# Attention exponentials turned by DMA instead of by TensorE in a pipelined attention and feed-forward block

## The chip, the cores and the metric

The kernel runs on one core of a Trainium2 chip. The metric is the device time of one execution in microseconds; lower is better. Before the change three runs gave 545.62, 542.62 and 543.9 us, median 543.9 us.

## The reference

There are 16 batches of 512 rows with 128 features. Per batch:

```python
x = x + _layernorm(attn(_layernorm(x)))      # attn: scores = (x*w_lhs) @ (x*w_rhs).T, softmax over rows, @ x
x = x + _layernorm(ffn(_layernorm(x)))
# ffn: h = silu(x@w1*s1) * (x@w2*s2)         128 -> 512
#      h = gelu(h@h1*sh1); h = gelu(h@h2*sh2)  512 -> 512 -> 512
#      y = h@w3*s3                            512 -> 128
```

The weights w1, w2, h1, h2 and w3 are ternary, all tensors are float32.

## The kernel before, in words

**Numbers in two halves.** A float32 value is kept as a high half and a low half, low = value - high. The feed-forward matmuls take fp32r halves, the product of attention weights and x takes fp16 halves. Each pair costs one rounding (the high half) and one subtraction on VectorE (the low half).

**Software pipeline.** Batches overlap. In step i five batches are at work (class `Stages`): `prep` = i+1 gets its first layer norm and is turned to features-first, `att` = i runs attention, `mid` = i-1 gets its second layer norm and is turned, `ffn` = i-2 runs the hidden layers, `tail` = i-3 runs the last layer and is stored. Attention of batches 0 and 1 is in `start()`, the last two batches' hidden layers in `finish()`. Steps 2 and 3 are written out, steps 4 to 14 are a loop, step 15 is written out. In the rest of the text a is the batch in attention, b the one in `mid`, f in `ffn`, g in `tail`.

**Order.** Nothing schedules the work but the text of the kernel: every engine has its own `step()` that lists its operations by hand, engines meet by semaphores, and an engine that waits holds all that is behind it. What the steps below need:

- TensorE (`pe`): `scores(a, j)` makes 128 query rows by 512 keys into one of two PSUM banks, `score_bank[j % 2]`, j = 0 to 3; it waits until `exp_done` says that the bank's earlier rows were read. `turn_e(a, j)` turns the 128 x 512 exponentials with four fp32 transposes into `eT_bank`. `attend(a, j)` multiplies them with x. `turn_x`, `turn_x2` and `turn_y` turn other tensors. `gated`, `layer1`, `layer2` and `layer3` are the feed-forward layers. Near the end of a step stand `attend(a, 0)`, `turn_e(a, 3)`, `turn_x2(b)`, `attend(a, 1)`, the last two `layer2` matmuls, `attend(a, 2)` and `attend(a, 3)`.
- ScalarE (`act`): `softmax(a, j)` is one Exp from the score bank to `exps` in float32, with the row sum. `high_e(a, j)` copies `eT_bank` to `eT_hi` (fp16). `silu`, `gelu1`, `gelu2`: the gelus are evaluated twice from PSUM, once for the value and once for the high half.
- VectorE (`dve`): `row_max(a, j)` on the scores, `low_e(a, j)` = `eT_bank` - `eT_hi`, one operand in PSUM, one in SBUF. `high_A` and `low_A` round and split the gated product, `low_B` and `low_C` split the gelus; these take both operands from SBUF. `aggregate(ln_x, prep)` finishes the statistics that GpSimd waits for.
- GpSimd (`pool`): in each step and in this order, `high_xn`, `rstd(ln_x)` and `normalize_x(prep)`, `rstd(ln_y)` and `shift_x1(g)`, `rstd(ln_x1)` and `normalize_x1(b)` which writes `x2n` for `turn_x2`, and the attention norm's constants. An `rstd` is four small operations that wait for each other: `var_eps`, `rstd` (a power of -0.5), `scaled_mean`, `shift`. In the profile ln_x1's tensors are shown as ln_x_..., x1 as x.
- SyncE (`sp`): loads of x, the store, and x1 saved and loaded again, one queue.

## Time and profile before

| | |
|---|---|
| median of three runs | 543.9 us (542.62 to 545.62) |
| span of the profiled execution | 548.2 us |
| that execution's time outside the profile | the records hold none; the three times above are the runs' |
| TensorE busy | 485.0 us (88%) |
| VectorE busy | 430.9 us (79%) |
| ScalarE busy | 393.2 us (72%) |
| GpSimd busy | 283.5 us (52%) |
| DMA, share of 16 engines | 12.6% |

Busy shares are means over stages, and TensorE's matmuls overlap each other in the records, so their starts tell more than their lengths. L12 is line 12 of the kernel. An operation is written "out<-in". "ISA" and "REGISTER_ALU" rows in listings of the program's order are waits and their register sums.

### The profile page before, as it was taken

Reading aid. Unit: us, or ns where it says so; the run is one execution under the profiler, and the core shown is the slowest. Engines: PE = TensorE matmul, PEld = TensorE weight load, DVE = VectorE, ACT = ScalarE, POOL = GpSimd, SP = SyncE. Lnnn points to the kernel's source line nnn. Section 1 sums busy time; section 2 is a strip of 40 time slices with the busy share of each in tenths; the row PEclk is TensorE's granted clock in tenths of the full one; section 3 lists DMA queues with packets and bytes.
Section 4 is the critical chain, followed back from the end, with each engine's and each line's share of the span. In section 5 each row is a group of like instructions: output and inputs, shape, how many; then the busy total and the mean of one; then the engine's idle time right before and its main releaser. Section 6 shows DMA issues by size and latency. Waiting matters only on the chain.

```text
span 548.2 us, 10143 instructions
## 1 busy us (share of the span) xinstructions
PE 485.0 (88%) x2818; PEld 386.8 (71%) x2818; DVE 430.9 (79%) x1160; ACT 393.2 (72%) x657; POOL 283.5 (52%) x568
## 2 busy tenths in 40 slices
PE   0765999999899989989898998989899998999992
PEld 0544777777777768777786877777777776877781
DVE  2873969889797978879697987969698797878762
ACT  3673777878697777868686786878678686875861
POOL 5364143837555472755547384655638365255332
PEclk9977999999999999999999999999999999999997
DMA  7010010100302020020202011020201102020111
GB/s 269 19 50 13 20 59 1 62 37 0 97 0 96 0 96 0 18 77 0 96 0 96 0 40 56 0 96 0 96 0 57 38 0 77 1 77 2 38 39 38
DMA packets 12549, 24.13 MB, mean 44 GB/s; under 512 B 1520, under 2 KB 1520, under 8 KB 12528
## 3 DMA queue, kind: packets, MB, share of 16 engines
q1 hardware_dynamic: 12528, 23.87, 12.6%
q8 instruction: 11, 0.18, 0.1%
q14 instruction: 10, 0.08, 0.0%
HBM read 11.28 MB, written 4.19 MB: 28 GB/s over the span
## 4 chain that ended last, share of the span: by engine, by line
PE 42%; POOL 30%; issue 14%; DVE 9%; ACT 2%; POOLq 2%; DMA 0%; DVEq 0%; SPq 0%
PE hid_bank L353 13%; PE hid_bank L277 10%; POOL x2n L1100 6%; PE score_bank L277 5%; POOL ln_x_rstd L1083 5%; PE mix_bank L277 5%; PE eT_bank L375 5%; POOL xn L1100 4%; POOL w_raw L1095 3%; POOL ln_y_rstd L1083 3%; POOL ln_x_shift L1088 2%; PE score_bank L282 2%; DVE hA_lo L777 2%; POOL ln_y_var_eps L1079 2%; POOL ln_x_scaled_mean L1085 2%
## 5 line engine op out<-in xcount | busy, mean ns | idle before, releaser
L628 ACT ACTIVATE w_raw<-hid_bank,columns 128x512 f32<-128x512 f32 x128 | 88.7, 693 | 25.6 <-PE hid_bank L353 21.0
L353 PE MATMUL hid_bank<-hA_hi,w_hi 128*128 128x512 f32 x256 | 104.6, 409 | 0.4 <-DVE w_raw L805 0.4
L353 PE MATMUL hid_bank<-hB_hi,w_hi 128*128 128x512 f32 x256 | 104.7, 409 | 0.0
L353 PE MATMUL hid_bank<-hA_lo,w_hi 128*128 128x512 f32 x256 | 101.0, 395 | 0.0
L353 PE MATMUL hid_bank<-hB_lo,w_hi 128*128 128x512 f32 x256 | 100.9, 394 | 0.0
L618 ACT ACTIVATE w_raw<-hid_bank,columns 128x512 f32<-128x512 f32 x64 | 43.6, 684 | 40.2 <-PE hid_bank L277 40.2
L777 DVE TENSOR_TENSOR hC_lo<-w_raw,hC_hi 128x512 fp32r<-128x512 f32 x64 | 45.7, 716 | 22.7 <-ACT hC_hi L629 22.6
L610 ACT CAST eT_hi<-eT_bank 128x512 f16<-128x512 f32 x64 | 37.9, 593 | 33.1 <-PE eT_bank L282 32.6
L1079 POOL TENSOR_SCALAR ln_x_var_eps<-ln_x_mean_var 128x4 f32<-128x4 f32 x32 | 9.5, 297 | 99.3 <-DVE ln_x_mean_var L790 98.0
L277 PE MATMUL hid_bank<-x2T_hi,w_hi 128*128 128x512 f32 x128 | 54.5, 426 | 3.7 <-issue 3.2
L805 DVE SCALAR_TENSOR_TENSOR w_raw<-hid_bank,columns,w_raw 128x512 f32<-128x512 f32 x64 | 47.7, 745 | 11.8 <-ACT w_raw L618 11.8
L353 PEld LDWEIGHTS hid_bank<-hA_hi,w_hi 128*128 128x128 f32 x256 | 48.2, 188 | 12.0 <-DVE w_raw L805 1.2
L353 PEld LDWEIGHTS hid_bank<-hB_hi,w_hi 128*128 128x128 f32 x256 | 48.2, 188 | 9.6
L353 PEld LDWEIGHTS hid_bank<-hB_lo,w_hi 128*128 128x128 f32 x256 | 48.3, 189 | 9.3
L777 DVE TENSOR_TENSOR hB_lo<-w_raw,hB_hi 128x512 fp32r<-128x512 f32 x64 | 45.7, 713 | 11.5 <-ACT hB_hi L629 11.5
L353 PEld LDWEIGHTS hid_bank<-hA_lo,w_hi 128*128 128x128 f32 x256 | 48.3, 189 | 8.8
L604 ACT ACTIVATE exps<-score_bank,neg_max 128x512 f32<-128x512 f32 x64 | 43.9, 687 | 13.7 <-DVE neg_max L795 10.9
L277 PE MATMUL hid_bank<-x2T_lo,w_hi 128*128 128x512 f32 x128 | 51.2, 400 | 2.5 <-issue 2.5
L777 DVE TENSOR_TENSOR eT_lo<-eT_bank,eT_hi 128x512 f16<-128x512 f32 x64 | 43.6, 681 | 4.4 <-ACT eT_hi L610 4.3
L282 PE MATMUL eT_bank<-ident,exps 128*128 128x128 f32 x256 | 40.1, 280 | 7.3 <-ACT exps L604 3.9
L277 PE MATMUL mix_bank<-xn_hi,eT_hi 128*128 128x128 f16 x256 | 46.3, 222 | 0.2 <-DVE eT_lo L777 0.2
L277 PE MATMUL mix_bank<-xn_hi,eT_lo 128*128 128x128 f16 x256 | 45.9, 220 | 0.0
(85 smaller groups left out, 1229.3 us busy)
## 6 DMA issues: line engine op xcount, KB each, us to landing
x_in<-x_dram SPq DMA_DIRECT2D x16, 256.0 KB, 2.8
x_res<-x_dram SPq DMA_DIRECT2D x16, 256.0 KB, 2.7
x_all<-x SPq DMA_DIRECT2D x16, 256.0 KB, 2.3
x_tail<-x_all SPq DMA_DIRECT2D x16, 256.0 KB, 2.8
out_dram<-w_raw SPq DMA_DIRECT2D x16, 256.0 KB, 2.0
w_raw<-weights_dram SPq DMA_DIRECT2D x5, 512.0 KB, 5.9
w_raw<-weights_dram SPq DMA_DIRECT2D x1, 256.0 KB, 7.3
columns<-columns_dram SPq DMA_DIRECT2D x1, 9.5 KB, 2.4
```

What stands on the lines that cost most here:

```text
L277: mm = nc.tensor.matmul(out, lhs, rhs, start=(n == 0), stop=(n == len(pairs) - 1))
L282: mm = nc.tensor.transpose(bank[:, t * P:(t + 1) * P], src[:, t * P:(t + 1) * P], ident[:, :])
L353: mm = nc.tensor.matmul(hid_bank[m][:, :], lhs, rhs, start=(k == 0 and n == 0), stop=(k == K - 1 and n == len(pairs) - 1))
L375: mm = nc.tensor.matmul(w3_bank[:, :], lhs, rhs, start=(k == 0 and n == 0), stop=(k == K - 1 and n == len(pairs) - 1))
L604: nc.scalar.activation(exps[:, j, :], score_bank[j % 2][:, :], ACT.Exp, bias=neg_max[:, j:j + 1], scale=-1.0, accum_out=row_sum[:, j:j + 1 ...
L610: nc.scalar.copy(eT_hi[:, j, :, :].rearrange("p t s -> p (t s)"), eT_bank[:, :]).then_inc(eT_hi_ready, 1)
L618: nc.scalar.activation(gate[:, m % 2, :], hid_bank[2 * (m % 2)][:, :], ACT.Silu, scale=columns[:, S1 + m:S1 + m + 1]).then_inc(gate_ready, 1)
L628: nc.scalar.activation(h_full[:, m, :], hid_bank[m][:, :], ACT.Gelu, scale=scale)
L777: return nc.vector.tensor_tensor(out, a, b, ALU.subtract)
L805: nc.vector.scalar_tensor_tensor(h_full[:, m, :], hid_bank[2 * (m % 2) + 1][:, :], columns[:, S2 + m:S2 + m + 1], gate[:, m % 2, :], ALU.m ...
L1083: nc.gpsimd.tensor_tensor(norm.rstd[:, :], norm.var_eps[:, :], minus_half[:, :], ALU.pow).then_inc(norm.chain, 1)
L1100: op = nc.gpsimd.tensor_scalar(out[:, t, :], src[:, t, :], norm.rstd[:, t:t + 1], norm.shift[:, t:t + 1], ALU.mult, ALU.add)
```

## The change

The exponentials are no longer turned by TensorE. ScalarE evaluates Exp twice from the score bank: once to fp16 (the high half, half 0 of `e_split`), once to float32 (`exps`, with the row sum). VectorE subtracts them, both from SBUF, to half 1 of `e_split`. Then SyncE's queue turns both halves of 128 x 512 at once with a DMA transpose of 128 x 1024 fp16 (256 KB) into `eT`, and `attend` waits for its landing. `eT_bank` and `high_e` are gone, and the bank is layer 3's alone. The order of SyncE and VectorE is written anew. The gated product is rounded and split by VectorE as before.

```diff
-        eT_hi = sb("eT_hi", [P, T, T, P], f16)
-        eT_lo = sb("eT_lo", [P, T, T, P], f16)
+        e_split = sb("e_split", [P, T, 2, S], f16)
+        eT = sb("eT", [P, T, 2, T, P], f16)
...
+            def turn_e(a, j):
+                sp.wait_ge(e_lo_ready, a * T + j + 1)
+                apart(sp)
+                wait_free(sp, pv_done, T, a, j + 1 - T)
+                apart(sp)
+                sp.dma_start_transpose(eT[:, j, :, :, :].rearrange("p h t s -> p (h t) s"),
+                                       e_split[:, j, :, :].rearrange("p h s -> p (h s)")).then_inc(eT_landed[j], 16)
...
-            def turn_e(b, j):
-                pe.wait_ge(exp_done, b * T + j + 1)
-                if j == 0:
-                    wait_free(pe, yT_ready, 1, b, -2)
-                wait_free(pe, eT_lo_ready, T, b, j)
-                turn(eT_bank, exps[:, j, :], eT_turned)
...
-                pe.wait_ge(eT_lo_ready, b * T + j + 1)
+                pe.wait_ge(eT_landed[j], b * 16 + 16)
...
-                wait_free(act, eT_turned, T, b, j + 1 - T)
+                wait_free(act, e_lo_ready, T, b, j + 1 - T)
                 if j == 0:
                     wait_free(act, rs_chain, 2, b, -1)
+                wait_free(act, eT_landed[j], 16, b, 0)
+                nc.scalar.activation(e_split[:, j, 0, :], score_bank[j % 2][:, :], ACT.Exp, bias=neg_max[:, j:j + 1],
+                                     scale=-1.0)
                 nc.scalar.activation(exps[:, j, :], score_bank[j % 2][:, :], ACT.Exp, bias=neg_max[:, j:j + 1],
                                      scale=-1.0, accum_out=row_sum[:, j:j + 1]).then_inc(exp_done, 1)
-
-            def high_e(b, j):
-                act.wait_ge(eT_turned, b * T + j + 1)
-                wait_free(act, pv_done, T, b, j + 1 - T)
-                nc.scalar.copy(eT_hi[:, j, :, :].rearrange("p t s -> p (t s)"), eT_bank[:, :]).then_inc(eT_hi_ready, 1)
...
             def low_e(b, j):
-                dve.wait_ge(eT_hi_ready, b * T + j + 1)
-                minus(eT_lo[:, j, :, :].rearrange("p t s -> p (t s)"), eT_bank[:, :],
-                      eT_hi[:, j, :, :].rearrange("p t s -> p (t s)")).then_inc(eT_lo_ready, 1)
+                dve.wait_ge(exp_done, b * T + j + 1)
+                minus(e_split[:, j, 1, :], exps[:, j, :], e_split[:, j, 0, :]).then_inc(e_lo_ready, 1)
```

**VectorE in a full step**, from the row maximum of j = 2 to the first `low_B`. Before (low_e is `eT_lo`, x1's statistics are ln_x_stats<-x):

```order
L795 TENSOR_REDUCE neg_max<-score_bank 128x1
L777 TENSOR_TENSOR hA_lo<-w_raw,hA_hi 128x512
L813 CAST hA_hi<-w_raw 128x512
L795 TENSOR_REDUCE neg_max<-score_bank 128x1
L790 BN_AGGR ln_x_mean_var<-ln_x_stats 128x2 x4
L777 TENSOR_TENSOR hA_lo<-w_raw,hA_hi 128x512
L849 SCALAR_TENSOR_TENSOR x<-mix_bank,ln_att_rstd,att_base 128x128 x4
L777 TENSOR_TENSOR xn_lo<-xn,xn_hi 128x512
L777 TENSOR_TENSOR eT_lo<-eT_bank,eT_hi 128x512
L782 BN_STATS ln_y_stats<-mix_bank 128x6 x4
L777 TENSOR_TENSOR hB_lo<-w_raw,hB_hi 128x512
```

Now, the same stretch (low_e is `e_split`):

```order
L777 TENSOR_REDUCE neg_max<-score_bank 128x1
L794 CAST hA_hi<-w_raw 128x512
L777 TENSOR_REDUCE neg_max<-score_bank 128x1
L759 TENSOR_TENSOR hA_lo<-w_raw,hA_hi 128x512
L772 BN_AGGR ln_x_mean_var<-ln_x_stats 128x2 x4
L759 TENSOR_TENSOR e_split<-exps,e_split 128x512
L830 SCALAR_TENSOR_TENSOR x<-mix_bank,ln_att_rstd,att_base 128x128 x4
L759 TENSOR_TENSOR e_split<-exps,e_split 128x512
L759 TENSOR_TENSOR xn_lo<-xn,xn_hi 128x512
L759 TENSOR_TENSOR e_split<-exps,e_split 128x512
L764 BN_STATS ln_y_stats<-mix_bank 128x6 x4
L759 TENSOR_TENSOR hB_lo<-w_raw,hB_hi 128x512
```

`aggregate(ln_x)` moved behind the last `low_A`, and three of the four `low_e` now stand between it and the first `low_B` (the fourth stands behind the second `low_B`); before, one did.

**ScalarE in a full step**, from Exp's table to the first gelu. Before:

```order
L604 ACT_TABLE_LOAD
L604 ACTIVATE exps,row_sum<-score_bank,neg_max 128x512 x2
L642 ACTIVATE w_raw<-eT_bank,columns 128x512
L604 ACTIVATE exps,row_sum<-score_bank,neg_max 128x512
L610 CAST eT_hi<-eT_bank 128x512
L604 ACTIVATE exps,row_sum<-score_bank,neg_max 128x512
L628 ACT_TABLE_LOAD
```

Now:

```order
L605 ACT_TABLE_LOAD
L605 ACTIVATE e_split<-score_bank,neg_max 128x512
L607 ACTIVATE exps,row_sum<-score_bank,neg_max 128x512
L605 ACTIVATE e_split<-score_bank,neg_max 128x512
L607 ACTIVATE exps,row_sum<-score_bank,neg_max 128x512
L640 ACTIVATE w_raw<-w_bank,columns 128x512
L605 ACTIVATE e_split<-score_bank,neg_max 128x512
L607 ACTIVATE exps,row_sum<-score_bank,neg_max 128x512
L605 ACTIVATE e_split<-score_bank,neg_max 128x512
L607 ACTIVATE exps,row_sum<-score_bank,neg_max 128x512
L626 ACT_TABLE_LOAD
```

All eight evaluations stand ahead of the gelu table; the copies that stood among the gelus are gone.

**SyncE in the loop's body.** Before:

```order
L226 DMA x_tail<-x_all 128x512
L229 REGISTER_ALU
L230 DMA out_dram<-w_raw 128x512
L221 ISA
L221 DMA x_all<-x 128x512
L217 ISA
L217 DMA x_res<-x_dram 128x512
```

Now:

```order
L217 DMA x_res<-x_dram 128x512
L233 ISA
L185 REGISTER_ALU
L237 DMA_TRANSPOSE eT<-e_split 128x8x128
L221 ISA
L221 DMA x_all<-x 128x512
L233 REGISTER_ALU
L185 REGISTER_ALU
L237 DMA_TRANSPOSE eT<-e_split 128x8x128
```

Two more transposes and the store follow. The store, which waits for the tail's result, is now last, and x1's save stands behind the first transpose.

## Rows read from the trace of the kernel before

**Rows 1.** The page: busy time of the engines, and the chain that ended last, by engine

```profile
PE 485.0 (88%) x2818; PEld 386.8 (71%) x2818; DVE 430.9 (79%) x1160; ACT 393.2 (72%) x657; POOL 283.5 (52%) x568
...
PE 42%; POOL 30%; issue 14%; DVE 9%; ACT 2%; POOLq 2%; DMA 0%; DVEq 0%; SPq 0%
```

**Rows 2.** ScalarE's timeline, silu table loads of steps 3 and 15: start, length (us)

```profile
82.42 1.28 ACT L615 ACT_TABLE_LOAD   x1
...
460.62 1.28 ACT L615 ACT_TABLE_LOAD   x1
```

**Rows 3.** Busy time of each engine in one full step

```profile
238.80:270.46 31.66, 29.59 (x180) 23.79 (x178) 26.46 (x72) 23.95 (x41) 17.89 (x35) 1.00 0.12 41
```

**Rows 4.** TensorE's timeline in that step: start, length; in brackets idle time and releaser

```profile
249.40 0.40 PE L277 MATMUL score_bank<-xT_hi,aT_lo 128*128 128x512 f32 x1
...
260.68 0.60 PE L282 MATMUL eT_bank<-ident,exps 128*128 128x128 f32 x4
...
261.04 0.47 PE L353 MATMUL hid_bank<-hB_hi,w_hi 128*128 128x512 f32 x1
...
265.07 0.61 PE L282 MATMUL eT_bank<-ident,exps 128*128 128x128 f32 x4
...
267.48 0.63 PE L282 MATMUL score_bank<-ident,x2n 128*128 128x128 f32 x4 [1.80 <-POOL x2n L1100]
```

**Rows 5.** Waits: engine, tile and line, releaser: total us, times, longest

```profile
PE score_bank L282 <- POOL x2n L1100: 20.5, 13, 1.8
```

**Rows 6.** VectorE's timeline in that step

```profile
250.21 0.68 DVE L795 TENSOR_REDUCE neg_max<-score_bank 128x1 f32<-128x512 f32 x1
...
250.81 0.37 DVE L790 BATCH_NORM_AGGREGATE ln_x_mean_var<-ln_x_stats 128x2 f32<-128x6 f32 x4
...
251.10 0.66 DVE L777 TENSOR_TENSOR hA_lo<-w_raw,hA_hi 128x512 fp32r<-128x512 f32 x1
...
252.71 0.68 DVE L777 TENSOR_TENSOR xn_lo<-xn,xn_hi 128x512 f16<-128x512 f32 x1
...
253.31 0.68 DVE L777 TENSOR_TENSOR eT_lo<-eT_bank,eT_hi 128x512 f16<-128x512 f32 x1
...
254.77 0.84 DVE L777 TENSOR_TENSOR hB_lo<-w_raw,hB_hi 128x512 fp32r<-128x512 f32 x1
...
256.88 0.69 DVE L777 TENSOR_TENSOR hB_lo<-w_raw,hB_hi 128x512 fp32r<-128x512 f32 x1 [0.40 <-ACT hB_hi L629]
...
258.27 0.68 DVE L777 TENSOR_TENSOR eT_lo<-eT_bank,eT_hi 128x512 f16<-128x512 f32 x1
```

**Rows 7.** GpSimd's timeline in that step

```profile
251.38 0.43 POOL L1079 TENSOR_SCALAR ln_x_var_eps<-ln_x_mean_var 128x4 f32<-128x4 f32 x1 [5.66 <-DVE ln_x_mean_var L790]
...
252.99 0.46 POOL L1085 TENSOR_TENSOR ln_x_scaled_mean<-ln_x_mean_var,ln_x_rstd 128x4 f32<-128x4 f32 x1
...
254.18 2.62 POOL L1100 TENSOR_SCALAR xn<-x_in,ln_x_rstd,ln_x_shift 128x128 f32<-128x128 f32 x4 [0.34 <-POOL ln_x_shift L1088]
...
256.88 0.74 POOL L1079 TENSOR_SCALAR ln_y_var_eps<-ln_y_mean_var 128x4 f32<-128x4 f32 x1
...
258.81 0.20 POOL L1085 TENSOR_TENSOR ln_y_scaled_mean<-ln_y_mean_var,ln_y_rstd 128x4 f32<-128x4 f32 x1
...
264.60 2.63 POOL L1100 TENSOR_SCALAR x2n<-x,ln_x_rstd,ln_x_shift 128x128 f32<-128x128 f32 x4 [0.31 <-POOL ln_x_shift L1088]
```

**Rows 8.** GpSimd's timeline in the start: the same four operations of xn

```profile
37.64 1.74 POOL L1100 TENSOR_SCALAR xn<-x_in,ln_x_rstd,ln_x_shift 128x128 f32<-128x128 f32 x4 [0.34 <-POOL ln_x_shift L1088]
```

**Rows 9.** ScalarE's timeline in that step, then its group of copies (busy, mean ns | idle)

```profile
246.67 0.69 ACT L604 ACTIVATE exps<-score_bank,neg_max 128x512 f32<-128x512 f32 x1
...
247.25 0.19 ACT L604 ACTIVATION_READ_ACCUMULATOR exps<-score_bank,neg_max 128x1 f32 x1
...
L610 ACT CAST eT_hi<-eT_bank 128x512 f16<-128x512 f32 x64 | 37.9, 593 | 33.1 <-PE eT_bank L282 32.6
```

**Rows 10.** DMA issues: KB each, median us from issue to landing

```profile
x_in<-x_dram SPq DMA_DIRECT2D x16, 256.0 KB, 2.8
...
w_raw<-weights_dram SPq DMA_DIRECT2D x1, 256.0 KB, 7.3
```

**Rows 11.** VectorE's timeline in the start: attention statistics of batch 0

```profile
28.82 0.89 DVE L782 BATCH_NORM_STATS2 ln_att_stats<-mix_bank 128x6 f32<-128x128 f32 x4
```

134 lines of the change are left out of this document (59 added, 75 removed).

## The prediction

> **What bounds the kernel now.** I read the page first. TensorE is busy 88% of the span, VectorE 79%, ScalarE 72%, GpSimd 52% [rows 1]. That suggests TensorE, and taking transposes from it would then pay at once. The chain that ended last says otherwise in the same rows: TensorE has 42% of it and GpSimd, the idlest, 30%. So I looked at one step. The silu table loads of steps 3 to 15 begin 378.2 us apart over 12 steps [rows 2], 31.5 us a step, and steps 5 to 14 look alike; the one from 238.80 to 270.46 took 31.66 us, with TensorE's records covering 29.59 [rows 3]. These 12 steps are two thirds of the time.
>
> In that step TensorE stands still at one place worth the name. It finishes `turn_e(a, 3)`, issued at 265.07, and then waits 1.80 us for `x2n` before `turn_x2` at 267.48 [rows 4]; over the kernel that wait counts 20.5 us in 13 times [rows 5]. Follow `x2n` back. GpSimd starts at 251.38, after 5.66 us of idleness that `aggregate(ln_x)` ends, and then runs ln_x, xn, ln_y, the tail's base, ln_x1 and `x2n` with no gap until 264.60 + 2.63 = 267.23 [rows 7]: 15.85 us in a row. `aggregate(ln_x)` begins at 250.81, right behind the last row maximum at 250.21 [rows 6], which needs the scores whose last matmul TensorE issued at 249.40 [rows 4]. So the loop is: TensorE from the step's start to the last scores (238.80 to 249.63, 10.8 us), VectorE (to 251.38, 1.75 us), GpSimd (15.85 us), TensorE's `turn_x2`, three `attend` and two matmuls (267.48 to 270.46, 3.0 us), and 0.25 us of hand-over. That is the step's 31.66. **None of the four `turn_e` lies in this loop**: the first follows the last scores, the last stands before the wait.
>
> **What is taken away.** One `turn_e` costs TensorE 0.36 us, from its start to the next instruction's (260.68 to 261.04) [rows 4]. Four are 1.44 us a step. They come off a stretch that ends in the 1.80 us of waiting, so the wait grows to about 3.2 us and the gain is 0. The cover is GpSimd's chain; if it went, 1.44 us a step would be paid out. `high_e`, four copies a step of 593 ns [rows 9], leaves ScalarE; in the steady step ScalarE waits there for TensorE, so nothing is gained.
>
> **What ScalarE gets.** One Exp holds ScalarE for 0.58 us (246.67 to the accumulator's read at 247.25 [rows 9]), and each `exp_done` now comes after two. The first comes 0.6 us later, so `scores(a, 2)` waits some 0.3 us, and `scores(a, 3)`, which needs the second, ends 0.4 us later in all. VectorE came late to that maximum anyway: the scores' last matmul was issued at 249.40 and takes 0.40 [rows 4], the maximum began at 250.21 [rows 6], 0.4 us after it. So only about 0.05 us reach the maximum.
>
> **What VectorE's new order costs.** `low_A(f, 3)` now stands ahead of `aggregate(ln_x)`. Such a subtraction holds VectorE for 0.60 us (252.71 to 253.31) [rows 6]. That delay goes into GpSimd's chain whole: **+0.6 us** a step, +0.65 with the 0.05.
>
> **What the new operands cost GpSimd.** This the diff hides. `low_e` took one operand from PSUM; now it takes both from SBUF. Compare the small operations of GpSimd, 0.20 us when undisturbed (258.81, while VectorE runs an `eT_lo` from PSUM since 258.27) [rows 6, 7]. `ln_x_scaled_mean` took 0.46 us while `xn_lo` ran from SBUF, and ended with it; `ln_y_var_eps` took 0.74 us beside an `hB_lo` that began in the same instant, 256.88 [rows 6, 7]. The four operations of `xn` took 2.62 us with two `hB_lo` beside them [rows 7], and 1.74 us undisturbed [rows 8]: 0.44 us lost per subtraction. The Trainium skill has this as a rule (SBUF — State Buffer, "Who interferes with whom"): a VectorE instruction with two SBUF inputs and a GpSimd instruction that reads SBUF exclude each other for the whole instruction, and one with at most one SBUF input does not. By that rule, the trace agrees, all four `low_e` change sides. They will stand at about 251.9, 253.5, 254.7 and 257.7 of that step's clock, all inside GpSimd's 15.85 us.
>
> The price of the four lies between two ends. The upper is 4 x 0.44 = 1.8 us a step. The lower is a small gain, -0.35 us: a `low_e` that falls on the 1.02 us power operations costs nothing, and they push the `hB_lo` to other places than the `var_eps` at 256.88 and the `shift` behind it, where two of these now cost 0.5 us each. Laid against the chain by hand: the first takes the place that `hA_lo` had, behind `aggregate`, where it costs the same 0.23 us; the second meets `scaled_mean` as `xn_lo` did; `xn_lo` then meets `shift`, +0.2; the third and the `hB_lo` cost `xn` up to 0.5 more; `ln_y` gets back up to 0.6; `x2n` meets the same two `hC_lo`, with one `shift` about 0.2 worse. I take **+0.25 us**, near the lower end, since the hand-laid order is the nearest thing to evidence. Sum per full step: 0.65 + 0.25 = **+0.9 us**, ends +0.3 and +2.4. Twelve steps: **+10.8 us** (+4 to +29).
>
> **What the transposes cost.** No row shows a DMA transpose. A plain load of the same 256 KB lands 2.8 us after issue; the slowest of that size 7.3 us, queued behind five others [rows 10]. I take about 3 us, nearest to the lone transfers. In the step there is room: the last `low_e` ends near 258.4, the last `attend` comes after 269. Moving x1's save behind the first transpose, and the store to the end of SyncE's queue, hides too: the save's data is needed two steps later, and the next load of x stood behind the store before, too.
>
> **Start and ends.** In the start there is no cover. All of batch 0's exponentials must be subtracted and landed before `attend(0, 3)`; before, that batch's statistics began at 28.82 [rows 11]. VectorE will be done with the subtractions near 25, plus 3 us, plus two `scores` of batch 1 that now stand ahead of the attends, 0.7 to 1.5 us each at that point: about 31. I put down **+2.5 us**, ends 0 and +6 (the latter if four transposes in a row need 2 us each on the queue). Step 2 waits at its first `layer2` for ScalarE, which reaches the gelus 1.1 us later (four Exps of 0.58, less one copy, and less waits), and gets two or three `turn_e` back: +0.5. Step 15 has no `prep`, and its chain runs over `turn_y`, whose statistics now stand behind three `low_e`: +0.7. `finish()` is unchanged.
>
> **Sum.** 10.8 + 2.5 + 0.5 + 0.7 = 14.5 us, on the profiled execution's span of 548.2 us: 562.7. The median of the runs is 543.9, so I forecast **558 us** in their terms; the 4.3 us between them stay.
>
> **Rivals.**
>
> *TensorE pays out.* If GpSimd's chain isn't the bound after all, or shrinks under the new order, the 1.44 us count: up to 14 x 1.44 = 20 us, **524 us**. For it: TensorE is busy 29.59 of 31.66 us [rows 3]. Against it: the wait of 1.80 us in 13 of the steps [rows 5], and nothing in the diff shortens GpSimd's 15.85. It decides as soon as `aggregate(ln_x)` to `x2n` gets shorter than 15.2 us, 0.65 less than now. 0.13.
>
> *The ports cost the upper end.* Each of the four `low_e` stops GpSimd for 0.44 us: +2.4 us a step, 29 us and 3.7 for the rest, **577 us**. For it: the rows of `xn` with and without company [rows 7, 8]. Against: the power operations are untouched. 0.12.
>
> *The transposes are slow.* Four must run between the end of the first `low_e`, near 252.6, and the last `attend`, near 269.9: from 4.3 us each, one after another, they become the bound. At the 7.3 us of [rows 10] they'd end at 281.8, 11.9 us late, 12 times 11.9 on 543.9: **687 us**. Against: that row is a transfer behind others. 0.07. The Trainium skill speaks against the change here (VectorE: DVE Perf Modes, "The three transpose paths"): 1309 ns by DMA against 390 ns on TensorE for 128 x 128 of two bytes; if eight such blocks added up, one transpose would take 10.5 us and the time would be some 700 us, an estimate from that page. No row here shows it.
>
> *Nothing to measure.* The hand-laid gains in ln_y cancel the 0.65: **544 us**. 0.10.
>
> The forecast itself has 0.58, with its own range of 547 to 570.
>
> **How the numbers follow.** A measurement here tells about 0.5% (2.7 us) from no change. Slower: 0.58 + 0.12 + 0.07 = 0.77, less 0.01 for the forecast's lower edge = 0.76. Same: 0.10, and that 0.01, 0.11. Faster: 0.13. The range of 541 to 577 leaves out the payout of TensorE and the slow transposes, 0.20.
>
> **What would show it.** Right: full steps of 32.3 to 33 us; the wait of TensorE on `x2n` up from 1.8 to about 3; GpSimd's chain from `ln_x_var_eps` to the end of `x2n` over 15.85 us, with small operations of 0.4 to 0.75 us beside `e_split`; `aggregate(ln_x)` 0.6 us later in the step. Wrong: steps under 31.5 us, a wait of TensorE on a DMA ahead of `attend`, `scores(a, 3)` late by over 1 us, or a GpSimd chain no longer than before.

## The result, and the profile after

The changed kernel takes 592.05 us, median of four runs (591.05 to 594.01), beside 544.66 us for the kernel before on the same chip (542.62 to 545.62): ratio 1.0865, 95% interval 1.0805 to 1.0925. The forecast was 558 us, with a range that ended at 577. The sign was right, and the loss is three times what was forecast: 47 us instead of 14.

The page of the changed kernel: busy time, the clock granted to TensorE in 40 slices, and the chain that ended last.

```profile
PE 487.1 (82%) x2562; PEld 374.1 (63%) x2562; DVE 427.9 (72%) x1160; ACT 392.9 (66%) x657; POOL 298.5 (50%) x568
...
PEclk9876879999797999989799998999798999999997
...
PE 37%; POOL 22%; issue 18%; DVE 12%; ACT 9%; POOLq 1%; ACTq 1%; DVEq 0%; DMA 0%; SPq 0%
```

Set against [rows 1] two things stand out. TensorE issues 256 matmuls fewer and is yet busy 2 us longer, and GpSimd, to which the change gave nothing to do, is busy 15 us longer. DMA has no share of the chain.

ScalarE's timeline gives the steps, as in [rows 2]: the silu table loads of steps 3 and 15.

```profile
94.38 1.28 ACT L613 ACT_TABLE_LOAD   x1
...
503.22 1.28 ACT L613 ACT_TABLE_LOAD   x1
```

The twelve full steps take 34.07 us each ((503.22 - 94.38) / 12), 2.55 more than in the profile of before; the forecast was 0.9 more. Together they are 30.6 of the 44.0 us between the two profiled executions. The start takes 7.8 us more (first silu table load at 52.78 instead of 44.97), step 2 takes 4.15 more and step 15 takes 1.4 more.

The view by windows: three full steps and a part of a fourth. Columns as in [rows 3]: busy time of PE, PEld, DVE, ACT and POOL, granted clock, DMA share, GB/s.

```profile
94.38:127.58 33.20, 28.85 (x162) 21.98 (x162) 26.37 (x72) 24.03 (x41) 19.47 (x35) 1.00 0.30 72
127.58:162.21 34.63, 31.21 (x162) 24.08 (x162) 26.22 (x72) 23.84 (x41) 18.17 (x35) 0.90 0.29 69
...
299.05:332.55 33.50, 28.66 (x162) 21.99 (x162) 26.38 (x72) 23.96 (x41) 19.33 (x35) 1.00 0.29 70
...
286.00:290.00 4.00, 4.00 (x12) 3.32 (x12) 1.85 (x4) 1.18 (x2) 3.23 (x8) 0.50 0.19 34
```

So there are two kinds of step. In the shorter one TensorE runs at its full clock throughout, the 2.4 GHz level, and the step is still 1.8 us longer than the one of [rows 3], with GpSimd busy 19.33 us instead of 17.89. In the longer one the granted clock falls to 0.50, the 1.2 GHz level, for some microseconds.

**The shorter kind.** VectorE's timeline of the step 299.05 to 332.55, from the last row maximum on:

```profile
310.53 0.69 DVE L777 TENSOR_REDUCE neg_max<-score_bank 128x1 f32<-128x512 f32 x1 [0.26 <-PE score_bank L299]
...
311.74 0.37 DVE L772 BATCH_NORM_AGGREGATE ln_x_mean_var<-ln_x_stats 128x2 f32<-128x6 f32 x4
...
313.64 0.68 DVE L759 TENSOR_TENSOR e_split<-exps,e_split 128x512 f16<-128x512 f32 x1
314.24 0.68 DVE L759 TENSOR_TENSOR xn_lo<-xn,xn_hi 128x512 f16<-128x512 f32 x1
314.85 0.68 DVE L759 TENSOR_TENSOR e_split<-exps,e_split 128x512 f16<-128x512 f32 x1
...
317.13 0.65 DVE L759 TENSOR_TENSOR hB_lo<-w_raw,hB_hi 128x512 fp32r<-128x512 f32 x1
317.71 0.68 DVE L759 TENSOR_TENSOR e_split<-exps,e_split 128x512 f16<-128x512 f32 x1
318.31 0.68 DVE L759 TENSOR_TENSOR hB_lo<-w_raw,hB_hi 128x512 fp32r<-128x512 f32 x1
```

GpSimd's timeline beside it:

```profile
312.31 0.43 POOL L1060 TENSOR_SCALAR ln_x_var_eps<-ln_x_mean_var 128x4 f32<-128x4 f32 x1 [6.50 <-DVE ln_x_mean_var L772]
...
313.93 1.66 POOL L1066 TENSOR_TENSOR ln_x_scaled_mean<-ln_x_mean_var,ln_x_rstd 128x4 f32<-128x4 f32 x1
...
316.32 3.68 POOL L1081 TENSOR_SCALAR xn<-x_in,ln_x_rstd,ln_x_shift 128x128 f32<-128x128 f32 x4 [0.34 <-POOL ln_x_shift L1069]
...
326.63 2.54 POOL L1081 TENSOR_SCALAR x2n<-x,ln_x_rstd,ln_x_shift 128x128 f32<-128x128 f32 x4 [0.31 <-POOL ln_x_shift L1069]
```

`ln_x_scaled_mean`, an operation of 0.20 us when undisturbed, took 0.46 in [rows 7] and takes 1.66 here. It was ready at 313.93 and ends at 315.59, just after the last of three subtractions that stand back to back from 313.64 to about 315.45. Three more such subtractions, 317.13 to 319.0, stand inside `xn`, which takes 3.68 us instead of 2.62 [rows 7] or 1.74 undisturbed [rows 8]. The whole chain, from `ln_x_var_eps` to the end of `x2n`, takes 16.86 us (312.31 to 329.17), 1.01 us more than before.

What TensorE waits for, in all of the kernel:

```profile
PE score_bank L304 <- POOL xn L1081: 58.1, 16, 11.5
...
PE score_bank L304 <- POOL x2n L1081: 12.5, 7, 3.0
PE hid_bank L368 <- DVE hB_lo L759: 10.3, 14, 0.7
```

The wait for `x2n` of [rows 5] has shrunk. In its place TensorE now waits at `turn_x` for `xn`, a place where it lost almost nothing before.

**The longer kind.** TensorE's timeline around `turn_x`, of the step 264.67 to 299.05 (mean clock 0.90) and, in the last line, of the step at 299.05; start and length, idle time in brackets:

```profile
285.77 1.11 PE L304 MATMUL score_bank<-ident,xn 128*128 128x128 f32 x4 [2.39 <-POOL xn L1081]
286.53 0.78 PE L368 MATMUL hid_bank<-hB_hi,w_hi 128*128 128x512 f32 x1
287.10 0.63 PE L368 MATMUL hid_bank<-hB_lo,w_hi 128*128 128x512 f32 x1
287.53 0.63 PE L368 MATMUL hid_bank<-hB_hi,w_hi 128*128 128x512 f32 x1
...
320.15 0.65 PE L304 MATMUL score_bank<-ident,xn 128*128 128x128 f32 x4 [2.38 <-POOL xn L1081]
```

In the step at 299.05 the same wait is 2.38 us, and behind it these matmuls start 0.23 us apart; here they start 0.43 us apart. Around `turn_x` the two steps differ in what the clock did after equal waits. The Trainium skill says that TensorE's clock falls to half when the engine is idle (TensorE: Matmul & The Clock Gate, "What's actually happening"). The trace agrees that the fall follows idle time, and it adds that equal waits of 2.4 us here bring the fall in some steps and not in others.

The DMA rows, issue to landing and then SyncE's own timeline:

```profile
eT<-e_split SPq DMA_TRANSPOSE x64, 3.1
```

```profile
312.95 1.27 SPq L237 DMA_TRANSPOSE eT<-e_split  x1
```

A transpose lands 3.1 us after its issue (forecast: about 3) and holds the queue for about 1.25 us. No wait of TensorE on a DMA stands among those of the page.

One remark on the profile of before. Its full steps come in two lengths too: two of the twelve take 30.7 us and the rest 31.7, all at full clock. Its span of 548.2 us is an execution on the long side, so differences of steps to it come out somewhat small. I judge versions by the ratio of their times, and use the lengths of steps to find the place.

### The profile page after: what moved, and what is told of

The parts are those of the page before. It is cut to its first block, busy times and chain, and to the rows that moved or that the text cites. A ratio compares the mean times of both kernels' runs of the same rounds, so it can differ in the third digit from the quotient of the medians.

```text
span 592.2 us, 9780 instructions
## 1 busy us (share of the span) xinstructions
PE 487.1 (82%) x2562; PEld 374.1 (63%) x2562; DVE 427.9 (72%) x1160; ACT 392.9 (66%) x657; POOL 298.5 (50%) x568
## 4 chain that ended last, share of the span: by engine, by line
PE 37%; POOL 22%; issue 18%; DVE 12%; ACT 9%; POOLq 1%; ACTq 1%; DVEq 0%; DMA 0%; SPq 0%
PE hid_bank L368 20%; PE score_bank L299 6%; DVE w_raw L786 4%; POOL xn L1081 4%; POOL ln_x_scaled_mean L1066 4%; POOL ln_x_rstd L1064 4%; PE mix_bank L299 4%; PE score_bank L304 3%; PE hid_bank L299 3%; POOL x2n L1081 2%; ACT L613 2%; DVE hA_lo L759 2%; ACT hC_hi L627 2%; POOL ln_y_rstd L1064 2%; ACT e_split L605 1%
## 5 line engine op out<-in xcount | busy, mean ns | idle before, releaser
L368 PE MATMUL hid_bank<-hB_hi,w_hi 128*128 128x512 f32 x256 | 115.7, 452 | 10.3 <-DVE hB_lo L759 10.3
L368 PE MATMUL hid_bank<-hB_lo,w_hi 128*128 128x512 f32 x256 | 110.8, 433 | 0.0
L368 PEld LDWEIGHTS hid_bank<-hB_hi,w_hi 128*128 128x128 f32 x256 | 55.5, 217 | 27.9 <-ACT hB_hi L627 14.9
L304 PE MATMUL score_bank<-ident,xn 128*128 128x128 f32 x64 | 15.4, 386 | 58.1 <-POOL xn L1081 58.1
L368 PEld LDWEIGHTS hid_bank<-hB_lo,w_hi 128*128 128x128 f32 x256 | 54.9, 215 | 11.5
L1081 POOL TENSOR_SCALAR xn<-x_in,ln_x_rstd,ln_x_shift 128x128 f32<-128x128 f32 x64 | 57.5, 907 | 5.4 <-POOL ln_x_shift L1069 5.4
L299 PE MATMUL mix_bank<-xn_hi,eT 128*128 128x128 f16 x512 | 52.2, 224 | 0.0
L304 PEld LDWEIGHTS score_bank<-ident,xn 128*128 128x128 f32 x64 | 9.9, 191 | 64.6 <-issue 42.4
L605 ACT ACTIVATE e_split<-score_bank,neg_max 128x512 f16<-128x512 f32 x64 | 44.0, 687 | 8.8 <-DVE neg_max L777 8.0
L777 DVE TENSOR_REDUCE neg_max<-score_bank 128x1 f32<-128x512 f32 x64 | 43.6, 683 | 6.6 <-PE score_bank L299 6.3
```

The costliest lines, as they stand in the source:

```text
L299: mm = nc.tensor.matmul(out, lhs, rhs, start=(n == 0), stop=(n == len(pairs) - 1))
L304: mm = nc.tensor.transpose(bank[:, t * P:(t + 1) * P], src[:, t * P:(t + 1) * P], ident[:, :])
L368: mm = nc.tensor.matmul(hid_bank[m][:, :], lhs, rhs, start=(k == 0 and n == 0), stop=(k == K - 1 and n == len(pairs) - 1))
L605: nc.scalar.activation(e_split[:, j, 0, :], score_bank[j % 2][:, :], ACT.Exp, bias=neg_max[:, j:j + 1], scale=-1.0)
L777: nc.vector.tensor_reduce(neg_max[:, j:j + 1], score_bank[j % 2][:, :], AX.X, ALU.min).then_inc(max_ready, 1)
L1081: op = nc.gpsimd.tensor_scalar(out[:, t, :], src[:, t, :], norm.rstd[:, t:t + 1], norm.shift[:, t:t + 1], ALU.mult, ALU.add)
```

## The experiments

A step's length below is the distance between silu table loads of a steady stretch. "Ratio" is to the kernel before on the same chip, with its 95% interval.

**1. One operand instead of two** (`e1_low_e_one_operand`)

```diff
-                minus(e_split[:, j, 1, :], exps[:, j, :], e_split[:, j, 0, :]).then_inc(e_lo_ready, 1)
+                nc.vector.tensor_reduce(e_junk[:, j:j + 1], exps[:, j, :], AX.X, ALU.min).then_inc(e_lo_ready, 1)
```

> The changed kernel, with each low_e replaced by a row minimum of exps: one operand from SBUF, about the same 0.68 us on VectorE, in the same place; the low half of the exponentials is left out (zeros). Theory A (VectorE instructions with two SBUF operands, back to back, shut GpSimd out: ln_x_scaled_mean 1.66 us and xn 3.68 us for four): scaled_mean falls to about 0.5, xn to about 2.7, xn is ready 2 us sooner, TensorE's wait before turn_x shrinks below 1 us, its granted clock stays at 1.00 in all full steps, and a full step takes 31.9 to 32.6 us instead of 34.1: some 565 us in all. Theory B (the moved aggregate and ScalarE's eight evaluations in a row make the loss): nothing changes by over 0.3 us a step, 590 us. Theory C (the DMA transposes make it): 590 us too.

Measured: 552.54 us, ratio 1.0105 (1.0056 to 1.0153). The same order, the same transposes, the same ScalarE, VectorE as busy as ever, and the loss shrinks from 8.65% to 1.05%. Full steps take 31.0 us at clock 1.00. Of the 7.6 points some 1.5 are the start and step 2, which get 7.9 us shorter in the profile. GpSimd's timeline in this run:

```profile
316.56 0.19 POOL L1061 TENSOR_SCALAR ln_x_var_eps<-ln_x_mean_var 128x4 f32<-128x4 f32 x1 [6.49 <-DVE ln_x_mean_var L773]
...
317.93 0.20 POOL L1067 TENSOR_TENSOR ln_x_scaled_mean<-ln_x_mean_var,ln_x_rstd 128x4 f32<-128x4 f32 x1
...
319.36 2.17 POOL L1082 TENSOR_SCALAR xn<-x_in,ln_x_rstd,ln_x_shift 128x128 f32<-128x128 f32 x4 [0.83 <-DVE xn_lo L760]
...
328.53 2.38 POOL L1082 TENSOR_SCALAR x2n<-x,ln_x_rstd,ln_x_shift 128x128 f32<-128x128 f32 x4 [0.31 <-POOL ln_x_shift L1070]
```

The chain takes 14.35 us (316.56 to 330.91). So four VectorE subtractions with two SBUF operands are what the loss hangs on; the transposes and the second Exp, which this run keeps, leave it at 1.05%. The row minimum differs from the subtraction in one more thing: it writes 128 numbers and not 128 x 512. Experiment 10 excludes that as the reason: there `low_e` writes as much as ever and has one operand in PSUM, and `xn` is undisturbed.

**2. The operand alone, in the kernel before** (`e3_before_two_sbuf`)

```diff
-                minus(eT_lo[:, j, :, :].rearrange("p t s -> p (t s)"), eT_bank[:, :],
+                minus(eT_lo[:, j, :, :].rearrange("p t s -> p (t s)"), exps[:, j, :],
```

> The kernel before, with low_e reading exps from SBUF instead of the transposed exponentials from PSUM, nothing else; the low halves are of the wrong values. The four low_e stand apart there. Theory A: each that meets GpSimd's chain at anything but a power operation costs it up to 0.6 us; the first (behind xn_lo, before a shift) and the second (before ln_y's scaled_mean) and the third (before ln_x1's scaled_mean) do: +0.5 to +1.5 us a step, 551 to 563 us. Theory B and C: 544 us.

Measured: 559.93 us, ratio 1.0222 (1.0175 to 1.0268), full steps of 32.06 us, GpSimd busy 18.94 us of one against 17.89 in [rows 3]. The same four operands from SBUF, spread as the kernel before spreads `low_e`, cost a quarter of what the change costs. GpSimd's chain in such a step takes 16.27 us. `ln_x_scaled_mean` takes 1.06 us there, beside `xn_lo` and a `low_e` in a row. This kernel subtracts the wrong values; its operations are of the same kind and size.

**3. The order alone, in the kernel before** (`e2_before_aggregate_later`)

```diff
-                if st.prep is not None:
-                    aggregate(ln_x, st.prep)
                 if f is not None:
                     low_A(f, 3)
+                if st.prep is not None:
+                    aggregate(ln_x, st.prep)
```

> The kernel before with one move of the change alone: aggregate(ln_x) behind the last low_A. The prediction priced this move at 0.6 us a full step, since it goes into GpSimd's chain whole: 7 us in all, ratio 1.010 to 1.015. Rival (the chain is no bound, or the moved operations rearrange GpSimd's collisions to its good): ratio 0.998 to 1.004.

Measured: 545.17 us, ratio 1.0001 (0.9976 to 1.0025). The forecast's largest term, 0.6 us a step, is nothing. GpSimd's timeline in this run, first and last operation of its chain:

```profile
312.95 0.20 POOL L1079 TENSOR_SCALAR ln_x_var_eps<-ln_x_mean_var 128x4 f32<-128x4 f32 x1 [6.25 <-DVE ln_x_mean_var L790]
...
325.06 2.56 POOL L1100 TENSOR_SCALAR x2n<-x,ln_x_rstd,ln_x_shift 128x128 f32<-128x128 f32 x4 [0.31 <-POOL ln_x_shift L1088]
```

The chain begins 0.6 us later in the step and takes 14.67 us (312.95 to 327.62) instead of 15.85: `hA_lo` is over before `ln_x_var_eps` begins (0.20 us, 0.43 in [rows 7]), and other collisions move as well.

**4. The place of `turn_x`** (`e4_turn_x_later`). 

```diff
                         layer2(general, f, (0,), (0,))
-                    if st.prep is not None:
-                        turn_x(st.prep)
...
                         layer2(general, f, (3,), (0,))
+                    if st.prep is not None:
+                        turn_x(st.prep)
```

> The changed kernel, with TensorE's turn_x of the next batch moved behind the 14 layer-2 matmuls that follow it in the order (3.3 us of work that does not need it). If TensorE's idle time there halves its clock in two steps of three and the slow stretch costs about 1 us a step (34.5 against 33.5 us), all full steps come to 33.5 us or a little less and the granted clock to 1.00: 7 to 9 us less, 583 us. If the clock falls for another reason, or x2n is all that counts, the time stays at 592 us.

Measured: 600.23 us, ratio 1.0969 (1.092 to 1.1019), slower than the changed kernel. The wait at `turn_x` is gone, and in the step looked at the one at `turn_x2` is 2.60 us, with the clock at 0.50 soon behind it.

**5. VectorE's order of before** (`e5_order_of_before`). The changed kernel with VectorE's `step()` in the order of the kernel before, which stands in the rows of order ahead of the prediction.

> The changed kernel with VectorE's order in the steps as before the change: aggregate(ln_x) ahead of the last low_A, one low_e behind low_xn, the others spread. The start keeps the new order. Theory A: with no three two-operand subtractions in a row, scaled_mean falls to 0.5 to 0.7 us, xn to 2.6 to 3, and the chain starts 0.7 us sooner; full steps of 31.8 to 32.8 us, 562 to 572 us. Theory B (ScalarE's evaluations): steps stay over 33.5 us. Theory C (the transposes): the last low_e now ends near the end of the step, so attend(a, 3) would wait for a landing 3 us behind it, and steps get longer than 34 us.

Measured: 601.46 us, ratio 1.1000 (1.0947 to 1.1053). The expectations of experiments 4 and 5 both failed, and both runs are slower than the changed kernel. TensorE's idle time had for the most part moved, from `turn_x` to `turn_x2`, and the clock fell there. From the timeline of TensorE in the run with the order of before:

```profile
329.95 1.09 PE L304 MATMUL score_bank<-ident,x2n 128*128 128x128 f32 x4 [2.82 <-POOL x2n L1081]
...
332.08 0.78 PE L368 MATMUL hid_bank<-hB_hi,w_hi 128*128 128x512 f32 x1
```

One `attend` and the two `layer2` matmuls behind it take 1.25 us and 1.00 us here, in the shorter step at 299.05 0.65 and 0.54 us. That made the clock a suspect of its own.

**6. TensorE kept busy ahead of `turn_x`** (`e10_tensore_kept_busy`)

```diff
+                wait_free(pe, exp_done, T, b, -1)
+                for _ in range(fill):
+                    nc.tensor.matmul(xT_bank[:, :], w_hi[:, 0:P], w_hi[:, 0:S], start=True, stop=True)
                 pe.wait_ge(xn_ready, b + 1)
-                wait_free(pe, exp_done, T, b, -1)
```

> The changed kernel with nine more matmuls of constants, 128x512, 0.23 us each, into the bank of turn_x while TensorE would wait for xn. They compute nothing that is used. Theory (in two of three steps the idle time ahead of turn_x lowers the granted clock to 0.50 for about 7 us and costs some 1 us): the granted clock stays 1.00 in the stretch behind turn_x, all full steps take about 33.5 us, 7 to 9 us less than the changed kernel, ratio 1.070 to 1.076. Rival (the clock's fall is covered by the wait for x2n and costs nothing): ratio 1.083 to 1.090, with the wait for x2n longer by what the clock gives back.

Measured: 582.31 us, ratio 1.0723 (1.0677 to 1.0769), as the theory had it. All full steps take 33.42 us, at clock 1.00:

```profile
290.82:324.24 33.42, 30.71 (x171) 23.70 (x171) 26.37 (x72) 23.97 (x41) 19.23 (x35) 1.00 0.29 71
```

1.4 points of the loss are the clock's: 34.07 - 33.42 = 0.65 us a step. GpSimd's chain in this run, first and last operation:

```profile
304.09 0.43 POOL L1062 TENSOR_SCALAR ln_x_var_eps<-ln_x_mean_var 128x4 f32<-128x4 f32 x1 [6.50 <-DVE ln_x_mean_var L774]
...
318.41 2.45 POOL L1083 TENSOR_SCALAR x2n<-x,ln_x_rstd,ln_x_shift 128x128 f32<-128x128 f32 x4 [0.31 <-POOL ln_x_shift L1071]
```

It takes 16.77 us, 2.42 more than in experiment 1, and the step is 2.42 us longer than there, both at clock 1.00. So the four operands' price reaches the step by way of this chain, and whole.

**7. The transposes doubled** (`e7_transposes_doubled`). 

```diff
+                sp.wait_ge(eT_landed[j], a * 32 + 16)
+                apart(sp)
+                sp.dma_start_transpose(eT[:, j, :, :, :].rearrange("p h t s -> p (h t) s"),
+                                       e_split[:, j, :, :].rearrange("p h s -> p (h s)")).then_inc(eT_landed[j], 16)
...
-                pe.wait_ge(eT_landed[j], b * 16 + 16)
+                pe.wait_ge(eT_landed[j], b * 32 + 32)
```

> The changed kernel with every DMA transpose done twice, one after the other, the second waiting for the first. Theory (the transposes are hidden behind other work in a full step): each row block lands 3.2 to 4.5 us later and the last still before its attend, so full steps change by less than 0.3 us; only the start grows, by 4 to 13 us, ratio to before 1.09 to 1.11. Rival (the transposes or SyncE's queue bound the step): steps longer by 3 us or more, ratio above 1.15.

Measured: 658.49 us, ratio 1.2124 (1.2071 to 1.2176), steps of 37.3 us. The expectation was wrong by its own arithmetic. Two in series hold the queue for about 4.7 us, so four pairs need some 19 us, and no more than that lies between the first transpose (312.95) and the last `attend` (331.7) of the changed kernel, with x1's save in the same queue. The wait is there to see:

```profile
PEld mix_bank L303 <- DMA eT<-e_split: 55.3, 22, 3.7
```

So this run tells how much room there is, not that the transposes bind: single ones are issued in 6.8 us (312.95 to 319.79), and the last lands near 321.7, ten microseconds ahead of its `attend`.

**8. An earlier aggregate, in the changed kernel and in the one before** (`e8_aggregate_early`, `e9_before_aggregate_early`). Both orders have `aggregate(ln_x)` right behind `x_statistics` and `low_xn` ahead of the last row maximum; the first also spreads `low_e` among operations on PSUM. Common to both, in VectorE's `step()`:

```diff
                     x_statistics(st.prep)
+                    aggregate(ln_x, st.prep)
                 if a is not None:
                     row_max(a, 2)
+                    low_xn(a)
```

> The changed kernel with VectorE's step in another order: aggregate(ln_x) right behind x_statistics and low_xn ahead of the third row maximum, so that GpSimd starts some 2.4 us earlier in the step, and the subtractions with two SBUF operands alternate with operations on PSUM. Theory (GpSimd's chain, lengthened by VectorE's subtractions from SBUF, sets the step): the chain ends about 2.4 us or more earlier, the waits of TensorE for xn and x2n nearly go, and the step falls from 34.07 us to what TensorE needs, 29.8 to 30.8 us; the whole kernel 540 to 556 us beside 548 before on one chip, ratio 0.985 to 1.015. Rival (the transposes by DMA or their issue on SyncE's queue set the step): the steps stay above 33 us, ratio 1.07 or more.

> The kernel before with the same two moves (aggregate(ln_x) behind x_statistics, low_xn ahead of the third row maximum; low_e stays from PSUM). If GpSimd's chain bounds the kernel before, as the prediction said, the wait of 1.8 us for x2n nearly goes: steps of 29.9 to 30.6 us, 12 to 22 us less in all, ratio 0.96 to 0.98. The rival that TensorE's own work is the bound: ratio 0.995 to 1.005. It also tells what freeing TensorE of four turn_e is worth where GpSimd's chain is no bound: then the other kernel of this call should have steps shorter than this one's by up to 1.44 us.

Measured: 577.17 us, ratio 1.0625 (1.0582 to 1.0669), steps of 33.25 us; and 540.71 us, ratio 0.9933 (0.9906 to 0.9960), steps of 30.72 us. Neither is in its expected range. The second **is faster than both kernels**, by 0.7% on the one before: its gain is real but a third of the least that was expected. With the chain begun 2 us earlier in the step TensorE still waits at `turn_x2`, since the chain got longer: `ln_x_rstd` and `ln_x_shift` collide now (1.67 and 0.73 us), and GpSimd waits 1.85 us for `ln_y`'s statistics. In the first the wait at `turn_x2` is 2.69 us, and 1.4 us after its end the clock falls to 0.50.

**9. The start alone** (`e13_start_reordered`). VectorE, TensorE and SyncE in another order ahead of step 2: `low_e` interleaved, the load of x behind two transposes, attends ahead of the next batch's scores.

> The changed kernel with another order in the start alone, on VectorE, TensorE and SyncE: the two low_e of batch 0 that can come early do, the next load of x stands behind two of its transposes, its attends ahead of batch 1's scores, its attention statistics ahead of two weight splits, and batch 1's attends ahead of turn_x2. Theory (of the 12 us that start and step 2 lost, 4 to 5 are order, 3 are GpSimd shut out by four subtractions in a row): 5 to 9 us less than the changed kernel, ratio to before 1.069 to 1.078, the first silu table load at 44 to 48 us instead of 52.8. Rival (the start loses by the transposes' own time, issue 1.25 us each and 3.1 us to land): 0 to 2 us less, ratio 1.083 to 1.087.

Measured: 587.25 us, ratio 1.0762 (1.0700 to 1.0824). The first silu table load comes at 49.75 instead of 52.78 and step 2 takes 38.6 instead of 41.6 us. Five to six of the twelve microseconds are the order's, the low end of what was expected; the table load was expected at 44 to 48.

**10. The exponentials kept in PSUM** (`e12_exps_in_psum`, `e11_statistics_first`). Both have experiment 9's start and a VectorE order of their own. The scores wait for `low_e` to free their bank. The edit of the operand:

```diff
-                nc.scalar.activation(exps[:, j, :], score_bank[j % 2][:, :], ACT.Exp, bias=neg_max[:, j:j + 1],
+                nc.scalar.activation(score_bank[j % 2][:, :], score_bank[j % 2][:, :], ACT.Exp, bias=neg_max[:, j:j + 1],
...
-                minus(e_split[:, j, 1, :], exps[:, j, :], e_split[:, j, 0, :]).then_inc(e_lo_ready, 1)
+                minus(e_split[:, j, 1, :], score_bank[j % 2][:, :], e_split[:, j, 0, :]).then_inc(e_lo_ready, 1)
```

> The changed kernel with that start, and with the float32 exponentials written back over the scores in their PSUM bank, so that low_e has one operand in SBUF; the bank comes free only after low_e, so low_e stands early in VectorE's step. x_statistics and aggregate(ln_x) stand ahead of the last row maximum. Theory (the port that VectorE's two-operand subtractions share with GpSimd is the main loss): GpSimd's small operations and xn are as short as in the kernel before, full steps of 30.0 to 31.2 us, 535 to 550 us beside 545 before, ratio 0.985 to 1.01. Rival (the time is lost by the longer way from scores to exponentials or by the transposes): steps above 32.5 us, ratio above 1.03.

> As the run with the exponentials in PSUM, with x_statistics at the very start of VectorE's step and aggregate(ln_x) ahead of the first low_e, so that GpSimd's chain starts 4 us earlier than in the changed kernel. If GpSimd's chain is then no bound, TensorE's work of about 28.9 us and the waits between it and ScalarE set the step: 29.5 to 30.5 us, ratio 0.965 to 0.99. If the 0.8 us ahead of the gated products goes into TensorE's first layer whole, steps of 30.5 to 31.2 us, ratio 0.99 to 1.0.

Measured: 584.94 us, ratio 1.0719 (1.0656 to 1.0783), and 585.08 us, ratio 1.0725 (1.0663 to 1.0787), steps of 34.1 us in both, outside both expected ranges. The theory's first half held: GpSimd is busy 17.06 us a step instead of 19.33, and `xn` takes 1.75 us, as undisturbed. The second half fell: the step is no shorter. In the first run GpSimd's chain begins hardly earlier (13.1 us after TensorE's start of the step instead of 13.4), since `scores(a, 2)` waits 0.94 us for `low_e` now; GpSimd then waits 1.44 us for `ln_y`'s statistics. In the second the chain begins 3 us earlier than in the first, waits 3.73 us for the same statistics, and nothing is gained. So `x2n` comes late enough for this (the first run: windows, then TensorE's timeline):

```profile
286.86:321.00 34.14, 30.19 (x162) 23.04 (x162) 26.43 (x72) 23.96 (x40) 17.06 (x35) 0.95 0.28 69
316.40:318.50 2.10, 2.09 (x16) 2.04 (x17) 0.27 (x1) 0.58 (x1) 0.19 (x1) 0.50 0.00 1
```

```profile
316.41 1.09 PE L303 MATMUL score_bank<-ident,x2n 128*128 128x128 f32 x4 [2.70 <-POOL x2n L1093]
```

**11. The same, with TensorE kept busy ahead of `turn_x2`** (`e17_busy_before_turn_x2`). 

```diff
+                for _ in range(fill):
+                    nc.tensor.matmul(x2T_bank[:, :], w_hi[:, 0:P], w_hi[:, 0:S], start=True, stop=True)
+                pe.wait_ge(x2n_ready, b + 1)
```

> The run with the exponentials in PSUM (ratio 1.072, steps 34.13 us), with nine more matmuls of constants, 128x512, 0.23 us each, where TensorE waits 2.70 us for x2n. They compute nothing that is used. Theory (what the change takes from TensorE lengthens that wait, the granted clock then falls to 0.5 and the attends and the first gated matmuls behind it take twice as long): the clock stays 1.00 and the steps fall by 1.2 to 2.0 us, ratio 1.028 to 1.045. Rival (the fall of the clock is covered by another chain): less than 0.4 us a step, ratio 1.063 to 1.075.

Measured: 569.32 us, ratio 1.0410 (1.0378 to 1.0442), steps of 32.54 us. `x2n` is as late as before, and the step is 1.6 us shorter all the same:

```profile
309.17 2.30 PE L338 MATMUL score_bank<-w_hi 128*128 128x512 f32 x9
311.87 0.66 PE L303 MATMUL score_bank<-ident,x2n 128*128 128x128 f32 x4 [0.41 <-POOL x2n L1095]
```

```profile
282.51:315.05 32.54, 30.88 (x171) 23.40 (x171) 26.43 (x72) 23.99 (x41) 17.09 (x35) 1.00 0.29 73
```

**12. The same fill under the order of before** (`e19_order_of_before_kept_busy`): experiment 5 with that edit.

> The run with VectorE's step order of the kernel before (ratio 1.100, steps 34.5 us), with nine idle matmuls of 0.23 us where TensorE waits 2.82 us for x2n. If that run missed its expectation because of the clock granted after that wait (attends and first gated matmuls at 0.5), as the runs on the changed kernel and with the exponentials in PSUM suggest, the steps fall by 1.2 to 1.8 us to 32.7 to 33.3 us, ratio 1.055 to 1.075. If it missed because the subtractions from SBUF cost GpSimd as much in this order too, and the clock is covered, ratio 1.09 to 1.105.

Measured: 582.73 us, ratio 1.0662 (1.0625 to 1.0699), steps of 33.27 us instead of 34.7. So 1.4 us of experiment 5's miss was the clock. The rest of it stands: 31.8 to 32.8 us had been expected, and with the clock at full in both, the order of before is about as good as the change's own (1.0662 against 1.0723, each with the fill at its place; the intervals overlap). GpSimd's chain tells why, with the last `attend` of the step below it:

```profile
338.61 0.43 POOL L1062 TENSOR_SCALAR ln_x_var_eps<-ln_x_mean_var 128x4 f32<-128x4 f32 x1 [5.53 <-DVE ln_x_mean_var L774]
...
340.23 1.06 POOL L1068 TENSOR_TENSOR ln_x_scaled_mean<-ln_x_mean_var,ln_x_rstd 128x4 f32<-128x4 f32 x1
...
352.23 3.11 POOL L1083 TENSOR_SCALAR x2n<-x,ln_x_rstd,ln_x_shift 128x128 f32<-128x128 f32 x4 [0.31 <-POOL ln_x_shift L1071]
```

```profile
358.27 0.23 PE L299 MATMUL mix_bank<-xn_hi,eT 128*128 128x128 f16 x1 [0.34 <-DMA eT<-e_split]
```

There is no row of three subtractions in this order. `ln_x_scaled_mean` and `xn` get 1.6 us shorter by it (1.06 and 2.72 us), and the later operations, `x2n` above all, get as much longer beside the subtractions that stand there now. The chain takes 16.73 us, against the 16.77 of experiment 6. Experiment 2 has the same order and operands in the kernel before, at 32.06 us a step. Of the 1.2 us between the two, 0.46 are the chain's (16.73 against 16.27), 0.36 its later begin in the step, and the rest lies behind it, where the last `attend` now waits 0.34 us for its transpose.

**13. GpSimd's norms exchanged** (`e15_x2n_before_ln_y`, `e18_sbuf_x2n_before_ln_y`, `e16_before_x2n_before_ln_y`). GpSimd makes `x2n` ahead of `ln_y`, and `turn_x2` moves up on the other engines; with `low_e` from PSUM, from SBUF, and in the kernel before. In GpSimd's `step()`:

```diff
-                if g is not None:
-                    rstd(ln_y, g)
-                    shift_x1(g)
                 if b is not None:
                     rstd(ln_x1, b)
                     normalize_x1(b)
+                if g is not None:
+                    rstd(ln_y, g)
+                    shift_x1(g)
```

> The same run (exponentials in PSUM) with GpSimd's two norms exchanged: ln_x1 and x2n ahead of ln_y and the tail's base, and turn_x2 with what follows it moved up accordingly on TensorE, ScalarE and VectorE. Theory (the wait for x2n and the fall of the clock behind it are all that keeps the full step above 31.5 us): no wait at turn_x2, the attends may wait up to 1 us for add_ffn, clock 1.00, steps of 30.3 to 31.3 us, ratio 0.98 to 1.005. Rival (the step is bound elsewhere by now, on VectorE's or ScalarE's order): steps above 32 us, ratio above 1.02.

> The same exchange with low_e as the change has it, both operands from SBUF, and the order of the run with the early aggregate. If the shared port costs GpSimd 1.5 to 2 us a step beside the run with the exponentials in PSUM, steps of 31 to 32.5 us, ratio 1.0 to 1.04; if scores that wait for low_e cost the other one as much, both are within 0.5% of each other.

> The kernel before, with the early aggregate and the same exchange on GpSimd. If GpSimd's chain to x2n was what bound it, as the prediction said, steps of 29.8 to 30.5 us, ratio 0.955 to 0.985. Beside the run with the exponentials in PSUM and the same exchange it tells what four turn_e less are worth on TensorE where it waits for nobody: up to 1.44 us a step for the other kernel.

Measured: 562.65 us, ratio 1.0292 (1.0261 to 1.0324), steps of 32.3 us; 572.78 us, ratio 1.0478 (1.0443 to 1.0512), steps of 33.1 us; 550.99 us, ratio 1.0083 (1.0054 to 1.0112), steps of 31.5 us. The wait at `turn_x2` is gone in all three, all three miss their expected ranges, and none beats the kernel before. The attends stand still 1.3 to 2.0 us a step instead. The views name no releaser there; by the program they wait for `add_ffn`, which ends 0.1 to 0.2 us before they begin and needs the tail's base, which GpSimd now makes last. Between the first two stands `low_e`'s operand, together with the order that goes with it: 1.8% in favour of PSUM, a part of it the clock's (1.00 in a step of the first, 0.95 in one of the second). The third, with the four `turn_e`, has a step 0.8 us shorter than the first, so their absence shows no gain; but the first has a wait of 0.95 us of the scores for `low_e` that the third has not, so this is no clean price of them.

## Why the prediction was wrong in size

**The bound: right for this change.** What GpSimd's chain loses the step loses (2.42 us in both, experiments 1 and 6), and taking 256 transposes from TensorE gained nothing. The rival that TensorE pays out (0.13) got no support: it was to decide once the chain is under 15.2 us, and with 14.35 in experiment 1 the step is 31.0 us, beside 31.1 in experiment 3, which has all four `turn_e`. The place was off: the wait at `turn_x2`, forecast to grow from 1.8 to about 3 us, is 1.43 us in the step at 299.05, and 2.38 us of waiting stand at `turn_x`. And the start of the chain isn't all that sets its end. Begun 1.4 to 3.5 us earlier (experiments 8 and 10) it waits for `ln_y`'s statistics, and where `x2n` comes early (experiment 13) the attends wait instead. All expectations that a shorter way to `x2n` gives steps of about 30 us failed.

**The early part of the step: right in kind, each term somewhat small.** Measured from TensorE's start of the step, the last scores' last matmul is issued 0.6 us later than before (forecast 0.4), the last row maximum begins at 11.64 us (310.53 - 298.89) instead of 11.41 (0.23 late, forecast 0.05), and `aggregate(ln_x)` 0.84 us later (forecast 0.65). With the chain's 1.01 us and the clock's 0.65 this makes 2.5 of the 2.55 us that a full step lost.

**The 0.6 us for the moved `aggregate`: wrong.** "That delay goes into GpSimd's chain whole" was the step. Alone it costs nothing (experiment 3), as the chain there is 1.2 us shorter than in the profile of before. The chain's length is not a constant to which a delay is added; it depends on what VectorE runs beside it.

**The 0.25 us for the four operands: wrong, and the step that failed.** Experiment 1 prices them at 7.6 points of the ratio, start included, of which 1.4 come by way of the clock. In full steps: 34.07 us, less 0.65 for the clock (experiment 6) is 33.42, less 31.0 (experiment 1) is 2.4 us for the operands, with the clock 3.1. Even the upper end, four times 0.44, was 1.8. The chain itself was to get 0.25 us longer and got 1.01. Two assumptions failed. One was "0.44 us lost per subtraction", that is, each subtraction stops GpSimd at most once and for what is left of it. Back to back they do more: the new order puts three in a row twice, and GpSimd, once shut out, waited for the whole row, 1.66 us for an operation of 0.20. The Trainium skill has the exclusion in the SBUF — State Buffer page, "Who interferes with whom"; it was cited, and the trace agrees. That a waiting GpSimd operation got no turn between back-to-back subtractions is in the rows of the step at 299.05. The other was that a `low_e` on a power operation costs nothing: `ln_y_rstd`, 1.02 us when undisturbed, takes 1.40 us from 320.36 on, beside an `hB_lo` begun at 320.22, and `ln_x_rstd` 1.67 us in the kernel before with an earlier aggregate. The rows of three are not the whole account, though: without them the same operands cost the chain as much (experiment 12, 16.73 us). The hand-laid gains near the lower end did not come in either order.

**The clock: not in the forecast at all.** The prediction counted TensorE's freed 1.44 us a step as "the wait grows, and the gain is 0". Below nothing it can be too: behind the longer waits of these runs the granted clock fell to 0.50, and the work there took about twice as long. It was worth 0.65 us a step in the changed kernel, 1.6 in experiment 11 and 1.4 in experiment 12. That the kernel before keeps its clock in spite of waits of 1.8 us is in [rows 3, 4]; one of its `turn_e` stands right ahead of that wait.

**The transposes: right.** About 3 us to land, no wait in the step of the changed kernel. The rival of slow transposes is out: one instruction for 128 x 1024 took 3.1 us. So is the estimate of the Trainium skill's page (VectorE: DVE Perf Modes, "The three transpose paths"), 10.5 us for eight blocks. Its "some 700 us" was also a wrong sum: four times 10.5 us from 252.6 end 24.7 us after 269.9, and by the prediction's own way that makes 840 us.

**The start: mis-sized.** Forecast +2.5 and +0.5 for step 2, measured +7.8 and +4.2. Batch 0's attention statistics were put "near 31" and come at 35.09: the four `low_e` in a row (21.92 to 24.5) make batch 1's `xn` 3.75 us long, SyncE's load of x stands ahead of the transposes and waits for that `xn`, so these are issued from 25.28, though the first was ready near 22.6. The waits queued in SyncE ahead of them were not priced. Experiment 9 gets half back by order. What the rest of the start is made of was not taken apart. Step 15, forecast +0.7, measured +1.4.

**Left open.** After the operands' cost is gone (experiment 1, ratio 1.0105) what is left stands in the profile at the start (first silu table load at 49.53 us instead of 44.97) and in step 15 (32.1 us instead of 29.9). No run had that kernel with the new start; experiments 10, 11 and the first of 13 had the new start and one operand in PSUM, but with scores that wait for `low_e`. Why the operands cost the chain the same in two so different orders was read from one step of each and not tested further. And no version with the transposes on DMA was found that beats its counterpart with them on TensorE.

## What to carry to other kernels

Before moving an operand from PSUM to SBUF on VectorE, list what GpSimd does beside it, and count every two-operand subtraction that falls into its chain. A row of them without a gap costs a GpSimd operation that meets it the whole row; but spreading them doesn't help as long as all still fall into the chain (16.73 us against 16.77 here). Work taken from TensorE ahead of a wait may be worth less than nothing; it lengthens the wait, and the clock behind a longer wait may cost more than the work did (1.44 us of `turn_e` a step here, 1.6 us of clock in experiment 11). A few idle matmuls in such a wait tell in one run whether it does.

## What the runs showed of the hardware that was not expected

- A GpSimd operation of 0.20 us took 1.66 us when it met three back-to-back subtractions of VectorE with both operands in SBUF.
- A GpSimd power operation of 1.02 us took 1.40 and 1.67 us where such a subtraction began near its start.
- Waits of TensorE of equal length, 2.38 and 2.39 us, were followed by a granted clock of 1.00 in one step and 0.50 in another of the same kernel; waits of 2.6 to 2.8 us were followed by 0.50 in the steps looked at, in experiment 8 only 1.4 us after work had begun again, and the wait of 1.80 us in the kernel before by 1.00.
- A DMA transpose of 128 x 1024 fp16 from SBUF to SBUF landed in 3.1 us, hardly more than a plain 256 KB transfer (2.6 us), while its issue held SyncE's queue for 1.25 us instead of about 0.35.
- ScalarE wrote the exponentials back to PSUM in 0.65 us where the write to SBUF took 0.68.
